# An attention and FFN kernel on one Trainium2 core: the sum of x and attention output moves from GpSimd to VectorE, a product and its row sum become one VectorE instruction, two small copies move to ScalarE

## The chip, the cores and the metric

One core of a Trainium2 chip runs the whole program. The metric is the time of one execution in device microseconds (us). Five engines work side by side and meet only through semaphores: TensorE (PE in the rows, with PEld for its weight loads), VectorE (DVE), ScalarE (ACT), GpSimd (POOL) and SyncE (SP, which here only issues DMAs). Each engine runs its instructions in the order in which they are written.

## The reference, cut to what matters

x and ctx are 16 batches of 128 x 1024 in float32. Each batch goes through an attention block and then through a feed-forward block (FFN) whose input is normalised over its 1024 features:

```python
x = x + xattn(layernorm(x), ctx, ctx)
x = x + ffn(layernorm(x))

def ffn(h):
    query = h @ Wq.T
    ... # router scores from query, top 8 of 256 slots, attention over them: aux_out
    aux_out = aux_out @ Wvd.T @ Wvu.T
    learned = (gelu(h @ Wu1.T + bu1) @ Wu2.T + bu2)[..., 0]
    u = clip(norm_var * 0.5 + sigmoid(learned) * 2.5, 0, 5)
    gate = sigmoid(gate_w1 * clip((u - 0.5) / 1.5, 0, 1) + gate_bias)
    return h + where(gate < 0.05, 0, gate) * aux_out
```

The change touches the first half of the FFN: the sum x + xattn in the layout that TensorE needs, the product with Wu1 and Wq (one matrix of 320 columns), gelu, the weighting with Wu2 and its sum over 256 units (`learned`), and `query`.

## The kernel before

The program is written by hand, engine by engine: a loop over `PERIODS` = 19 periods of four sub-steps (i = 0 to 3) pipelines the attention over the 16 batches, and ends in the FFN. In period 17 (`B + 1`) the FFN's first half begins: `hidden_step(b)` is called on TensorE, VectorE and ScalarE for b = 0 to 7 from sub-steps of periods 17 and 18 (`early_step`), for b = 8 to 16 from a loop of its own behind the periods. Step b works on batch b with the batch before and the one after it. After step 16 comes the second half (top 8, weights, output), which the change leaves as it is.

For each batch b the first half is this chain, with the engine and the line:

- SP: `load_hx` (L422) loads x transposed into one of three buffers `hx`, `load_ho` (L428) the attention output from DRAM into one of two buffers `ho`. `load_hx(n)` waits until batch n-3 has been split (`hT_lo_done`), `load_ho(n)` until batch n-2 has been added (`h_added`). They alternate in one queue.
- GpSimd: `h_add` (L1133), hx = hx + ho, 128x1024.
- ScalarE: `hT_high` (L901) rounds hx to the matmul's format (`hT_hi`); VectorE: `hT_low` (L1304) takes the rest (`hT_lo` = hx - `hT_hi`).
- TensorE: `hidden_products` (L627), 24 matmuls of 320 columns into one half of `k_slot`.
- VectorE: `unit_bias` (L1313) scales 256 of those columns and adds bu1; `query_rows` (L1318) scales the other 64 into `q_rows`.
- TensorE: `query_transpose` (L637) turns `q_rows`; VectorE: `query_copy` (L1322) moves the result to `query`.
- ScalarE: `unit_gelu` (L905); VectorE: `unit_weights` (L1326) multiplies by Wu2; ScalarE: `unit_sum` (L909) sums the product into `learned`.

VectorE's step b is, in this order, hT_low(b+1), unit_weights(b-1), unit_bias(b), query_rows(b), query_copy(b-1). ScalarE's is hT_high(b+1), unit_gelu(b-1), `hidden_sum(b)` (L895, a 128x1024 pass over x that the output needs later), unit_sum(b-1). TensorE's is hidden_products(b), query_transpose(b-1).

Other work lies in between in steps 0 to 8: on TensorE the last products of the attention (`o_pair`, L574) and the turns of its output (`o_turn`, L585); on GpSimd `norm_scale` (L1092 to L1100) and small chains for the normalisation (`rstd2_pow`, L1120 to L1127); on VectorE `residual` (L1291) and `statistics` (L1297) of the last three batches; later the split of Wvu (`WvuT_hi` on VectorE, L1503; `WvuT_lo` on GpSimd, L1205), and on ScalarE a logarithm that needs another function table (L921).

Before that, in period 16, VectorE, ScalarE, GpSimd and TensorE end the softmax of q: `q_shift` (L1258, L1264), exponent on ScalarE (L811), `q_reciprocal` (L1271, L1275), `q_scale` on GpSimd (L1081), `q_turn` on TensorE (L527).

Of the kernel before, what the change touches and what calls it, by code (L numbers as in the profile page):

```python
# [57 lines left out]
def attention_ffn_kernel(nc, x, x_cols, ctx_rows, ctx_cols, WqT_raw, WkT_raw, Wv_rows, WoT_rows, bo_row, g_row, Wuq_cols,  # L58
# [3 lines left out]
    with ctx:  # L62
# [284 lines left out]
        gelu_weighted = sem("gelu_weighted")  # L347
# [32 lines left out]
        def has(b):  # L380
            return 0 <= b < B
# [397 lines left out]
        def _(act):  # L779
# [127 lines left out]
            def unit_sum(b, k):  # L907
                act.wait_ge(gelu_weighted, b + 1)
                nc.scalar.activation(units[:, k, :], units[:, k, :], ACT.Identity,  # L909
                                     accum_out=learned[:, b, :]).then_inc(learned_done, 1)  # L910

            def hidden_step(b):
                if b + 1 < B:
                    hT_high(b + 1, (b + 1) % 2)
                if has(b - 1):
                    unit_gelu(b - 1, (b - 1) % 2)
                if has(b):
                    hidden_sum(b)
# [3 lines left out]
                if 0 < b < B:  # L922
                    unit_sum(b - 1, (b - 1) % 2)
# [110 lines left out]
            for i in range(1, B + 2):  # L1034
                if has(i - 1):
                    softmax_exp(i - 1, (i - 1) % 2)
                if i == 1:
                    unit_sum(B - 1, (B - 1) % 2)
# [16 lines left out]
        def _(pool):  # L1055
# [73 lines left out]
            def h_add(b):  # L1129

                pool.wait_ge(hx_in[b % HX], 16 * (b // HX + 1))
                pool.wait_ge(ho_in[b % 2], 16 * (b // 2 + 1))
                nc.gpsimd.tensor_tensor(hx[:, b % HX, :], hx[:, b % HX, :], ho[:, b % 2, :], ALU.add).then_inc(h_added, 1)  # L1133

# [25 lines left out]
            for b in range(PERIODS):  # L1160
                p, o, e = b - 1, b - 2, b - 3
                for i in range(4):
# [19 lines left out]
                    if b == B and i == 2:  # L1182
                        h_add(0)
                    if b == B + 1 and i == 0:
                        h_add(1)
# [3 lines left out]
                    if early_step(b, i) >= 0:  # L1189
                        h_add(early_step(b, i) + 2)  # L1190
# [9 lines left out]
            for b in range(EARLY, B):  # L1200
                if b + 2 < B:
                    h_add(b + 2)
# [16 lines left out]
        def _(dve):  # L1219
# [80 lines left out]

            def hT_low(b, k):
# [14 lines left out]
            def query_rows(b, k):  # L1316
                wait(dve, rows_T, b - 1)
                V.tensor_scalar_mul(q_rows[:, k, 0:BOT], unit_psum(b)[:, UH:UQ], rstd2[:, b, :]).then_inc(rows_copied, 1)  # L1318

            def query_copy(b, k):  # L1320
                dve.wait_ge(rows_T, b + 1)
                V.tensor_copy(query[:, b, :], query_psum(b)).then_inc(query_done, 1)  # L1322

            def unit_weights(b, k):
                dve.wait_ge(gelu_done, b + 1)
                V.tensor_tensor(units[:, k, :], units[:, k, :], Wu2[:, :], ALU.mult).then_inc(gelu_weighted, 1)  # L1326
# [267 lines left out]
```

## Time and profile before

| what | value |
|---|---|
| runs | 633.19 us median of 3 (632.27 to 635.33) |
| the profiled execution | 632.16 us |
| its span, first to last instruction | 630.3 us |
| mean granted TensorE clock | 0.984 |
| busy: TensorE, VectorE, ScalarE, GpSimd | 590.2 us (94%), 563.4 (89%), 418.3 (66%), 471.9 (75%) |
| first product of the FFN starts | at 491.87 us |
| last product of the FFN's first half starts | at 577.92 us |

The profile gives the start and length of every instruction. A length counts from the moment at which the instruction is at the head of its engine with its semaphores fulfilled, so it can hold time in which the instruction itself can't go on. Times of places are counted from the start of the span.

### The profile page before, as it was taken

Reading aid. Unit: us, or ns where it says so; the run is one execution under the profiler, and the core shown is the slowest. Engines: PE = TensorE matmul, PEld = TensorE weight load, DVE = VectorE, ACT = ScalarE, POOL = GpSimd, SP = SyncE. Lnnn points to the kernel's source line nnn. Section 1 sums busy time; section 2 is a strip of 40 time slices with the busy share of each in tenths; the row PEclk is TensorE's granted clock in tenths of the full one; section 3 lists DMA queues with packets and bytes.
Section 4 is the critical chain, followed back from the end, with each engine's and each line's share of the span. In section 5 each row is a group of like instructions: output and inputs, shape, how many; then the busy total and the mean of one; then the engine's idle time right before and its main releaser. Section 6 shows DMA issues by size and latency. Waiting matters only on the chain.

```text
span 630.3 us, 11307 instructions
## 1 busy us (share of the span) xinstructions
PE 590.2 (94%) x3606; PEld 511.0 (81%) x3606; DVE 563.4 (89%) x722; ACT 418.3 (66%) x864; POOL 471.9 (75%) x437
## 2 busy tenths in 40 slices
PE   4999999999999999999999999999897996789896
PEld 3768888888888888888888888888776986777574
DVE  5999999999999999999999999999879449987996
ACT  5556657676767676775777676767654565466783
POOL 4953569797797979797978879797848897761394
PEclk9999999999999999999999999999999899989899
DMA  7949697978889697978787886967695875550156
GB/s 299 251 128 241 187 216 218 228 205 211 226 201 234 200 241 203 239 204 214 219 224 216 208 229 184 238 226 175 183 280 196 246 258 180 187 200 1 43 226 266
DMA packets 70441, 131.33 MB, mean 208 GB/s; under 512 B 12032, under 2 KB 44448, under 8 KB 68080
## 3 DMA queue, kind: packets, MB, share of 16 engines
q1 hardware_dynamic: 57184, 101.16, 55.1%
q10 hardware_dynamic: 12304, 27.01, 16.6%
q0 software_dynamic: 896, 2.45, 1.2%
q8 instruction: 29, 0.48, 0.4%
q14 instruction: 28, 0.23, 0.1%
HBM read 63.47 MB, written 33.55 MB: 154 GB/s over the span
## 4 chain that ended last, share of the span: by engine, by line
PE 76%; DVE 7%; issue 5%; POOL 5%; ACT 3%; DMA 2%; SPq 1%; ACTq 0%; DVEq 0%; POOLq 0%
PE ob L574 16%; PE gm L543 16%; PE q_slot L501 5%; PE k_slot L501 4%; PE q_slot L503 4%; PE k_slot L503 4%; PE k_slot L502 4%; PE q_slot L502 4%; PE turn L527 4%; PE k_slot L627 2%; PE gm L552 2%; PE turn L585 2%; POOL hx L1133 2%; DVE units L1326 2%; PE turn L747 1%
## 5 line engine op out<-in xcount | busy, mean ns | idle before, releaser
L1081 POOL TENSOR_TENSOR qs_sb<-qs_sb,qrec 128x1024 f32<-128x1024 f32 x64 | 121.8, 1903 | 82.5 <-DVE qrec L1275 82.3
L574 PEld LDWEIGHTS ob<-mt_sb,q_hd 128*128 128x128 f32 x1024 | 124.5, 194 | 6.7 <-issue 2.6
L574 PE MATMUL ob<-mt_sb,q_hd 128*128 128x128 f32 x1024 | 128.1, 279 | 1.1 <-ACT q_hd L816 1.1
L543 PE MATMUL gm<-ekT,ctxT 128*128 128x256 f32 x512 | 118.2, 379 | 0.0
L543 PEld LDWEIGHTS gm<-ekT,ctxT 128*128 128x128 f32 x512 | 96.0, 190 | 13.6
L811 ACT ACTIVATE qs_sb<-qs_sb 128x1024 f32<-128x1024 f32 x64 | 68.0, 1062 | 47.6 <-DVE qs_sb L1264 46.6
L801 ACT ACTIVATE ek<-k_slot,nkm 128x1024 f32<-128x1024 f32 x62 | 69.1, 1115 | 32.2 <-DVE nkm L1239 31.8
L1239 DVE TENSOR_REDUCE nkm<-k_slot 128x1 f32<-128x1024 f32 x62 | 74.1, 1195 | 14.6 <-PE k_slot L503 14.6
L1271 DVE TENSOR_REDUCE qsum<-qs_sb 128x16 f32<-128x1024 f32 x64 | 77.2, 1206 | 3.7 <-ACT qs_sb L811 2.8
L1264 DVE TENSOR_TENSOR qs_sb<-q_slot,qm 128x1024 f32<-128x1024 f32 x64 | 78.4, 1224 | 2.2
L1246 DVE STREAM_TRANSPOSE kt<-ek 128x1024 f32<-128x1024 f32 x64 | 79.0, 1234 | 0.0
L1258 DVE TENSOR_REDUCE qm<-q_slot 128x16 f32<-128x1024 f32 x64 | 75.9, 1186 | 0.5 <-issue 0.5
L501 PE MATMUL k_slot<-ctx_hi,WkT_hi 128*128 128x512 f32 x124 | 54.7, 441 | 8.1 <-DVE ctx_lo L1439 7.3
L627 PE MATMUL k_slot<-WuqT_hi,hT_hi 128*128 128x320 f32 x128 | 43.0, 336 | 14.0 <-issue 14.0
L501 PE MATMUL q_slot<-WqT_hi,xn_hi 128*128 128x512 f32 x128 | 52.9, 413 | 1.9 <-DVE qs_sb L1264 1.8
L1133 POOL TENSOR_TENSOR hx<-hx,ho 128x1024 f32<-128x1024 f32 x16 | 42.3, 2646 | 12.5 <-DMA ho<-o_turned 12.5
L503 PE MATMUL q_slot<-WqT_lo,xn_hi 128*128 128x512 f32 x128 | 50.3, 393 | 0.0
L502 PE MATMUL q_slot<-WqT_hi,xn_lo 128*128 128x512 f32 x128 | 50.0, 391 | 0.0
L807 ACT COPY g_sb<-gm 128x512 f32<-128x512 f32 x16 | 9.4, 591 | 60.8 <-PE gm L543 60.8
L503 PE MATMUL k_slot<-ctx_lo,WkT_hi 128*128 128x512 f32 x124 | 49.2, 397 | 0.0
L502 PE MATMUL k_slot<-ctx_hi,WkT_lo 128*128 128x512 f32 x124 | 49.1, 396 | 0.0
L1304 DVE TENSOR_TENSOR hT_lo<-hx,hT_hi 128x1024 fp32r<-128x1024 f32 x16 | 28.9, 1809 | 19.6 <-ACT hT_hi L901 19.6
(192 smaller groups left out, 1385.9 us busy)
## 6 DMA issues: line engine op xcount, KB each, us to landing
ekT<-kt SPq DMA_DIRECT2D x488, 64.0 KB, 3.1
q_turned<-qt SPq DMA_DIRECT2D x16, 1024.0 KB, 4.8
q_hd<-q_turned ACTq DMA_DIRECT2D x64, 256.0 KB, 6.2
ctx_in<-ctx_rows SPq DMA_DIRECT2D x16, 512.0 KB, 6.1
x_all<-x SPq DMA_DIRECT2D x16, 512.0 KB, 4.9
ctxT<-ctx_cols SPq DMA_DIRECT2D x16, 512.0 KB, 5.7
o_turned<-o_sb ACTq DMA_DIRECT2D x16, 512.0 KB, 3.1
hx<-x_cols SPq DMA_DIRECT2D x16, 512.0 KB, 3.5
```

The source lines that it names most:

```text
L501: nc.tensor.matmul(dst, lhs[0], rhs[0], start=True, stop=False)
L502: nc.tensor.matmul(dst, lhs[1], rhs[0], start=False, stop=False)
L503: return nc.tensor.matmul(dst, lhs[0], rhs[1], start=False, stop=True)
L543: last = nc.tensor.matmul(gm[:, cols], ctxT[:, b % 2, j, :], ekT[:, 2 * half:2 * half + 2, :, j * BLK:(j + 1) * BLK], start=(j == 0), stop ...
L574: last = nc.tensor.matmul(ob[:, (j % 4) * C:(j % 4 + 1) * C], q, mt_sb[:, b % 2, t, :], start=(t == 0), stop=(t == T - 1))
L801: nc.scalar.activation(ek[:, i % 2, :], k_psum(b, i)[:, :], ACT.Exp, bias=nkm[:, i:i + 1], accum_out=ksum[:, b % 2, i:i + 1]).then_inc(k_e ...
L1081: nc.gpsimd.tensor_tensor(e, e, qrec[:, i % 2, :].unsqueeze(2).broadcast_to([P, PAIR, DH]), ALU.mult).then_inc(q_mul, 1)
L1239: V.tensor_reduce(nkm[:, i:i + 1], k_psum(b, i)[:, :], AX, ALU.max, negate=True).then_inc(k_max, 1)
L1246: V.transpose(kt[:, i, :], ek[:, i % 2, :]).then_inc(k_T, 1)
L1258: V.tensor_reduce(qm[:, :], q, AX, ALU.max).then_inc(q_max, 1)
L1264: V.tensor_tensor(qs_sb[:, i % 2, :].rearrange("p (m d) -> p m d", d=DH), q, qm[:, :].unsqueeze(2).broadcast_to([P, PAIR, DH]), ALU.subtra ...
L1271: V.tensor_reduce(qsum[:, :], qs_sb[:, i % 2, :].rearrange("p (m d) -> p m d", d=DH), AX, ALU.add).then_inc(q_sum, 1)
```

## The change

- `h_add` is issued by VectorE, in step b behind hT_low(b+1), for batch b+2; batches 0 and 1 are added in periods 16 and 17. GpSimd no longer has it.
- `unit_weights` is `tensor_tensor_reduce`: product with Wu2 and the sum over 256 columns into `learned`. It appears as two instructions, the product and a read-out of one column. `unit_sum` on ScalarE is gone, with its semaphore.
- `query_rows` and `query_copy` are issued by ScalarE, one step later than VectorE issued them: query_rows(b-1) behind hT_high(b+1), query_copy(b-2) behind unit_gelu(b-1).

The diff, without the lines that only take the old functions away:

```diff
 # ScalarE
+            def query_rows(b, k):
+                act.wait_ge(units_biased, b + 1)
+                act.wait_ge(rstd2_done, b + 1)
+                wait(act, rows_T, b - 1)
+                nc.scalar.mul(q_rows[:, k, 0:BOT], unit_psum(b)[:, UH:UQ], rstd2[:, b, :]).then_inc(rows_copied, 1)
+
+            def query_copy(b, k):
+                act.wait_ge(rows_T, b + 1)
+                nc.scalar.copy(query[:, b, :], query_psum(b)).then_inc(query_done, 1)
 
             def hidden_step(b):
                 if b + 1 < B:
                     hT_high(b + 1, (b + 1) % 2)
                 if has(b - 1):
+                    query_rows(b - 1, (b - 1) % 2)
                     unit_gelu(b - 1, (b - 1) % 2)
+                if has(b - 2):
+                    query_copy(b - 2, b % 2)
                 if has(b):
                     hidden_sum(b)
...
-                if 0 < b < B:
-                    unit_sum(b - 1, (b - 1) % 2)
...
                 if i == 1:
-                    unit_sum(B - 1, (B - 1) % 2)
+                    query_copy(B - 1, (B - 1) % 2)
                     act.wait_ge(learned_done, B)
 # GpSimd
-                    if b == B and i == 2:
-                        h_add(0)
-                    if b == B + 1 and i == 0:
-                        h_add(1)
...
-                    if early_step(b, i) >= 0:
-                        h_add(early_step(b, i) + 2)
...
-                if b + 2 < B:
-                    h_add(b + 2)
 # VectorE
+            def h_add(b):
+
+                dve.wait_ge(hx_in[b % HX], 16 * (b // HX + 1))
+                dve.wait_ge(ho_in[b % 2], 16 * (b // 2 + 1))
+                V.tensor_tensor(hx[:, b % HX, :], hx[:, b % HX, :], ho[:, b % 2, :], ALU.add).then_inc(h_added, 1)
...
             def unit_weights(b, k):
                 dve.wait_ge(gelu_done, b + 1)
-                V.tensor_tensor(units[:, k, :], units[:, k, :], Wu2[:, :], ALU.mult).then_inc(gelu_weighted, 1)
+                V.tensor_tensor_reduce(units[:, k, :], units[:, k, :], Wu2[:, :], 1.0, 0.0, ALU.mult, ALU.add,
+                                       learned[:, b, :]).then_inc(learned_done, 1)
...
                 if b + 1 < B:
                     hT_low(b + 1, (b + 1) % 2)
+                if b + 2 < B:
+                    h_add(b + 2)
...
                 if b < B:
                     unit_bias(b, b % 2)
-                    query_rows(b, b % 2)
-                if has(b - 1):
-                    query_copy(b - 1, (b - 1) % 2)
...
                     if b == B + 1 and i == 0:
                         hT_low(0, 0)
+                        h_add(1)
...
+                    if b == B and i == 2:
+                        h_add(0)
```

VectorE's order at the first addition, in period 16: `q_shift` of sub-step 2 (qm, qs_sb), then `q_reciprocal` (qsum, qrec). Before:

```order
L1258 TENSOR_REDUCE qm<-q_slot 128x16
L1264 TENSOR_TENSOR qs_sb<-q_slot,qm 128x1024
L1271 TENSOR_REDUCE qsum<-qs_sb 128x16
L1275 RECIPROCAL qrec<-qsum 128x16
L1284 STREAM_TRANSPOSE qt<-qs_sb 128x2x4x4x32
```

And with the change:

```order
L1249 TENSOR_REDUCE qm<-q_slot 128x16
L1255 TENSOR_TENSOR qs_sb<-q_slot,qm 128x1024
L1296 TENSOR_TENSOR hx<-hx,ho 128x1024
L1262 TENSOR_REDUCE qsum<-qs_sb 128x16
L1266 RECIPROCAL qrec<-qsum 128x16
L1275 STREAM_TRANSPOSE qt<-qs_sb 128x2x4x4x32
```

The addition of batch 0 (hx<-hx,ho) has come between the two, ahead of all that VectorE still does for q.

VectorE's step 10 of the FFN, one of the steps with nothing else in them. Before:

```order
L1304 TENSOR_TENSOR hT_lo<-hx,hT_hi 128x1024
L1326 TENSOR_TENSOR units<-units,Wuq_in 128x256
L1313 SCALAR_TENSOR_TENSOR units<-k_slot,rstd,Wuq_in 128x256
L1318 TENSOR_SCALAR q_rows<-k_slot,rstd 128x64
L1322 COPY query<-q_slot 128x128
```

And with the change:

```order
L1301 TENSOR_TENSOR hT_lo<-hx,hT_hi 128x1024
L1296 TENSOR_TENSOR hx<-hx,ho 128x1024
L1315 ISA units,learned<-units,Wuq_in 128x256
L1315 ISA learned 128x1
L1310 SCALAR_TENSOR_TENSOR units<-k_slot,rstd,Wuq_in 128x256
```

The addition stands behind hT_lo, the product has its read-out behind it, and the two small copies are gone from VectorE.

ScalarE at the end of the first half (steps 15 and 16 and the first exponent of the second half, L1015). Before:

```order
L905 ACTIVATE units<-units 128x256
L1015 ACT_TABLE_LOAD
L1015 ACTIVATE w_sb,wsum<-logits,nlmax 128x256
L909 ACTIVATE units,learned<-units 128x256
L1041 ACTIVATE ga<-learned,half 128x16
```

And with the change:

```order
L910 ACTIVATE q_rows<-k_slot,rstd 128x64
L904 ACTIVATE units<-units 128x256
L914 COPY query<-q_slot 128x128
L1020 ACT_TABLE_LOAD
L1020 ACTIVATE w_sb,wsum<-logits,nlmax 128x256
L914 COPY query<-q_slot 128x128
L1046 ACTIVATE ga<-learned,half 128x16
```

Two copies stand ahead of that exponent now and one behind it, where the sum stood.

## Rows read from the trace of the kernel before

**Rows 1.** The table by stretch: engines' busy time (count), granted clock, DMA share, GB/s.

```profile
526.70:578.00 51.30, 39.58 (x234) 37.02 (x234) 44.98 (x67) 30.96 (x52) 29.93 (x20) 0.93 0.44 154
...
526.68:530.40 3.72, 3.72 (x26) 3.59 (x25) 3.23 (x4) 1.24 (x3) 3.39 (x5) 1.00 0.61 170
...
534.10:539.30 5.20, 5.18 (x25) 5.14 (x25) 5.20 (x7) 2.90 (x5) 2.38 (x1) 0.67 0.54 207
...
551.00:556.20 5.20, 5.16 (x25) 5.16 (x25) 4.47 (x5) 2.70 (x5) 5.20 (x3) 0.67 0.56 202
```

**Rows 2.** Instructions grouped by line, 526.7 to 578 us: count, busy, mean ns, idle before.

```profile
L627 PE MATMUL k_slot<-WuqT_hi,hT_hi 128*128 128x320 f32 x73 | 25.0, 342 | 11.7 <-issue 11.7
...
L1304 DVE TENSOR_TENSOR hT_lo<-hx,hT_hi 128x1024 fp32r<-128x1024 f32 x9 | 17.1, 1894 | 4.2 <-ACT hT_hi L901 4.2
...
L1326 DVE TENSOR_TENSOR units<-units,Wuq_in 128x256 f32<-128x256 f32 x10 | 13.0, 1297 | 0.5 <-ACT units L905 0.5
...
L901 ACT CAST hT_hi<-hx 128x1024 fp32r<-128x1024 f32 x9 | 9.3, 1037 | 1.9 <-POOL hx L1133 1.9
L1313 DVE SCALAR_TENSOR_TENSOR units<-k_slot,rstd,Wuq_in 128x256 f32<-128x256 f32 x10 | 4.7, 475 | 0.5 <-PE k_slot L627 0.5
L909 ACT ACTIVATE units<-units 128x256 f32<-128x256 f32 x10 | 4.2, 416 | 20.4 <-DVE units L1326 20.4
...
L1322 DVE COPY query<-q_slot 128x128 f32<-128x128 f32 x10 | 2.8, 277 | 0.0
...
L909 ACT ACTIVATION_READ_ACCUMULATOR units<-units 128x1 f32 x10 | 1.9, 187 | 0.0
...
L921 ACT ACT_TABLE_LOAD x1 | 1.3, 1283 | 0.0
```

**Rows 3.** TensorE's instructions in order of time: start, length, idle before.

```profile
534.12 0.38 PE L627 MATMUL k_slot<-WuqT_hi,hT_hi 128*128 128x320 f32 x1 [3.58 <-issue]
```

**Rows 4.** The same view for VectorE, then GpSimd, at two places.

```profile
530.69 3.33 DVE L1304 TENSOR_TENSOR hT_lo<-hx,hT_hi 128x1024 fp32r<-128x1024 f32 x1 [0.77 <-ACT hT_hi L901]
...
562.00 2.63 DVE L1326 TENSOR_TENSOR units<-units,Wuq_in 128x256 f32<-128x256 f32 x1
...
530.60 2.35 POOL L1133 TENSOR_TENSOR hx<-hx,ho 128x1024 f32<-128x1024 f32 x1
...
561.49 2.86 POOL L1133 TENSOR_TENSOR hx<-hx,ho 128x1024 f32<-128x1024 f32 x1 [2.43 <-DMA ho<-o_turned]
```

**Rows 5.** The chain of waits, 574 to 590 us: start, length, engine and line.

```profile
576.20 1.72 PE turn L643 x4
577.92 3.52 PE k_slot L627 x24
...
585.05 0.42 PE turn L737 x2
```

**Rows 6.** The same timeline, other work of steps 7 to 10: VectorE, GpSimd.

```profile
535.07 1.21 DVE L1291 TENSOR_TENSOR x_all<-turn,x_all 128x1024 f32<-128x1024 f32 x1
...
540.28 1.27 DVE L1297 BATCH_NORM_STATS2 st<-x_all 128x6 f32<-128x512 f32 x2
...
543.08 1.22 DVE L1304 TENSOR_TENSOR hT_lo<-hx,hT_hi 128x1024 fp32r<-128x1024 f32 x1
...
553.14 2.57 POOL L1205 TENSOR_TENSOR WvuT_lo<-Wuq_in,WvuT_hi 128x1024 fp32r<-128x1024 f32 x1
```

**Rows 7.** The same timeline at the first addition: VectorE, GpSimd, TensorE.

```profile
480.07 1.22 DVE L1271 TENSOR_REDUCE qsum<-qs_sb 128x16 f32<-128x1024 f32 x1 [1.34 <-ACT qs_sb L811]
...
477.99 1.90 POOL L1081 TENSOR_TENSOR qs_sb<-qs_sb,qrec 128x1024 f32<-128x1024 f32 x1
...
486.24 1.09 PE L527 MATMUL turn<-ident,qs_sb 128*128 128x128 f32 x8 [2.60 <-DVE x_all L1291]
```

**Rows 8.** Lines again, 491.9 to 582 us: all products of the first half.

```profile
L627 PE MATMUL k_slot<-WuqT_hi,hT_hi 128*128 128x320 f32 x128 | 43.0, 336 | 14.0 <-issue 14.0
```

**Rows 9.** DMA issues, 526.7 to 578 us: count, KB, median us to landing.

```profile
ho<-o_turned SPq DMA_DIRECT2D x7, 512.0 KB, 4.2
```

More of the change, by code:

```diff
@@ L346, in attention_ffn_kernel @@
         gelu_done = sem("gelu_done")
-        gelu_weighted = sem("gelu_weighted")
         learned_done = sem("learned_done")
@@ L905, in unit_gelu @@
                 nc.scalar.activation(units[:, k, :], units[:, k, :], ACT.Gelu_apprx_tanh).then_inc(gelu_done, 1)
[L907 to L910, printed above, removed]
+            def query_rows(b, k):
[6 more added lines that the diff above has]
+                nc.scalar.copy(query[:, b, :], query_psum(b)).then_inc(query_done, 1)
             def hidden_step(b):
@@ L1127, in rstd2_pow @@
                 nc.gpsimd.tensor_scalar(one_rstd2[:, b, :], rstd2[:, b, :], 1.0, None, ALU.add).then_inc(one_rstd2_done, 1)
[L1129 to L1133, printed above, removed]
             nc.gpsimd.memset(half_neg[:, :], -0.5).then_inc(consts, 1)
@@ L1314, in unit_bias @@
                                        ALU.mult, ALU.add).then_inc(units_biased, 1)
[L1316 to L1322, printed above, removed]
             def unit_weights(b, k):
                 dve.wait_ge(gelu_done, b + 1)
-                V.tensor_tensor(units[:, k, :], units[:, k, :], Wu2[:, :], ALU.mult).then_inc(gelu_weighted, 1)
+                V.tensor_tensor_reduce(units[:, k, :], units[:, k, :], Wu2[:, :], 1.0, 0.0, ALU.mult, ALU.add,
+                                       learned[:, b, :]).then_inc(learned_done, 1)
             def log_mean():
```

## The prediction

> **What bounds the kernel now.** I read the table by stretch first, and in it the stretch from step 6 to the end of step 14 of the FFN's first half, where every engine has work but none is full: TensorE works 39.58 of 51.30 us, VectorE 44.98 [rows 1]. The groups by line say where TensorE stands: all its idle time, 11.7 us, lies ahead of the first matmul of a product, put down to "issue" [rows 2]. That product waits for hT_lo. The longest is the 3.58 us before 534.12 [rows 3], a tenth of a us after hT_lo's end (530.69 + 3.33 = 534.02 [rows 4]). A product with its transpose takes 3.72 us without a wait, and 5.2 us in the two stretches where the granted clock is 0.67 [rows 1]: the engine ran at its lower level (1.2 GHz) for most of those products, and at the higher (2.4 GHz) where the row says 1.00. The first of the two begins right behind the wait that ends at 534.12.
>
> So hT_lo is late, and why is the point of the case. hT_low on VectorE takes 1894 ns in the mean and the product with Wu2 1297 ns, though it has a quarter of the columns [rows 2]. The timeline shows them beside h_add on GpSimd: h_add runs from 530.60 to 532.95; hT_low, at the head from 530.69, ends at 534.02, 1.07 us after h_add. Again: h_add ends at 564.35, the product with Wu2 at 564.63, 0.28 us after it [rows 4]. VectorE's instruction with two SBUF inputs does nothing until GpSimd's is through, and then needs 1.1 us (1024 columns) or 0.3 us (256). It also holds up what follows: the sum on ScalarE waits 20.4 us in all for the product [rows 2], and behind that sum in ScalarE's order stands the next hT_high, for which the next hT_low waits. The ring hT_high, hT_low, product, sum, hT_high sets the pace, not TensorE.
>
> **The change, part by part.**
>
> h_add on VectorE. The trace has no such addition there; the nearest row is hT_low, same shape, two SBUF inputs, 1.1 us of its own [rows 4]; the far end is GpSimd's 2.35. I take 1.1. What it removes is the collision: GpSimd has no large work left in most steps.
>
> The fused product. Nothing in the trace is like it. The low end is the plain product, 0.3 us [rows 4]; the near high end adds to the 0.3 a whole pass of the length of ScalarE's sum with its read-out, 0.416 + 0.187 [rows 2], 0.9 in all. I take 0.5, the plain product with a read-out like ScalarE's, since the list of instructions has just these two. A far worse price is a rival below. ScalarE's wait for the product goes with the sum.
>
> VectorE's step is then 1.1 + 1.1 + 0.5 + 0.48 (unit_bias) = 3.2 us, ScalarE's about what it was: 30.96 / 10 = 3.1 us [rows 1, 2], less 0.6 for the sum, plus two copies at no more than VectorE's 0.28 each [rows 2]. Both are below TensorE's 3.72. The ring that is left, hT_high 1.04, hT_low 1.1, h_add 1.1, is 3.3 with its hand-overs: below it as well. I cost the two copies on ScalarE at nothing: query_rows(b-1) stands behind the hT_high that the next product needs anyway, and hT_low takes longer than the copy. That cover goes where ScalarE is late, below.
>
> So the steady step is TensorE's, 3.72. From the start of product 6 (526.68) to that of product 15 (577.92) [rows 1, 5] it was 51.24 us. Nine products are 33.5, with the 1.72 of the scores [rows 5] 35.2. The waits of 11.7, two products at the lower clock (1.5 each) and 1.3 of small gaps make up the rest. In the changed kernel TensorE will still wait where VectorE, with 0.5 us of slack a step, has other work:
> - step 8, behind residual, 1.21 [rows 6]: 0.7 us;
> - step 9, behind the statistics, whose chain runs from 540.28 to 543.08, 2.8 us [rows 6]: 2.3 us;
> - step 11, where GpSimd's WvuT_lo, 2.57 [rows 6], stops VectorE as h_add did: 2.3 us;
> - steps 13 and 14, where ScalarE loads a function table twice, 1.28 each [rows 2], and the logarithm's mean is formed: 0.7 each.
>
> That is 6.7; the stretch is 41.9 and the gain 9.3. Whether the lower clock comes back is open: one of its two came behind a wait of 3.58 [rows 3], and mine are 2.3. At worst it adds 1.5 twice, at best nothing.
>
> The entry. h_add(0) now stands ahead of q_reciprocal. VectorE was idle there for 1.34 us until 480.07, but GpSimd's q_scale runs until 479.89 [rows 7] and holds the addition off; it ends at 481.0, and q_reciprocal starts 0.9 us late. Behind it in VectorE's order stand the last q_shift and residual, for which TensorE already waits 2.60 us at 486.24 [rows 7]: TensorE is 0.9 us late into the FFN. Some comes back: of the waits for hT_lo (14.0 in the whole half, 11.7 in the stretch [rows 2, 8]) 2.3 us lie in steps 0 to 5. I expect 0.6 back, since behind them ScalarE's squares of the last batch and GpSimd's norm_scale, which o_turn awaits, are hardly earlier. Net +0.3 at product 6, between -1.4 (all back) and +0.9 (none).
>
> The exit. The second half's first transpose starts 3.6 us after the last product ends (585.05 [rows 5]). ScalarE's two copies ahead of the exponent delay it by some 0.45; the copy behind it takes the place of VectorE's. I take +0.2, between 0 and +0.8. From there on nothing is changed. GpSimd's queue loses the additions alone; its norm_scale of batch 14 comes earlier, and nobody waits for that.
>
> The queues: SP's loads wait for hT_low(n-3) and h_add(n-2), both now in VectorE's order. A load of ho lands 4.2 us after its issue [rows 9], and its buffer is free two steps less an addition before it is needed, 2 x 3.72 - 1.1 = 6.3. It fits, with 2.1 to spare; but an addition that waits for a load would now stop all of VectorE, where it stopped GpSimd alone.
>
> Sum: -9.3 + 0.3 + 0.2 = -8.8. The profiled execution took 632.16 us, 1.0 under the median of 633.19; against the median the forecast is **624.4 us**. With the bounds (0.3 to 0.9 for the fused product, clock, entry, exit) this case spans 620.5 to 629.
>
> **The rivals.**
>
> *TensorE is the bound throughout.* VectorE may catch up on the four places, since a late hT_lo costs only what exceeds the product that runs meanwhile. Then the 6.7 us of waits go too: 624.4 - 6.7 = 617.7. For it: hT_low is ready more than a us before TensorE needs it in a plain step. Against: GpSimd's WvuT_lo holds VectorE for longer than that.
>
> *VectorE is simply full.* The Trainium skill, "Perfetto Trace Analysis", section "Optimizing Scalar/DVE Operations", warns that GpSimd and VectorE share an SBUF read port, so that moving work between the two might not help. As a mechanism of this kernel, in rows: VectorE is busy 44.98 of the 51.30 us [rows 1]; nine additions at 1.22 [rows 6] add 11.0, ten pairs of copies take away 5.5, ten read-outs add 1.9 [rows 2]: 52.4, which is 1.1 more than the stretch, so 633.19 + 1.1 = 634.3, no change. Against it: the 44.98 holds the waits for GpSimd, (1.894 - 1.1) x 9 + (1.297 - 0.3) x 10 = 17 us [rows 2, 4], which end with the collision. The trace speaks against that rule here, as the shared time itself shrinks (2.4 us on GpSimd becomes 1.1 on VectorE).
>
> *Slower: the fused instruction is dear.* It stands in the middle of VectorE's step, ahead of unit_bias, which frees TensorE's target. The other three take 2.7 us, the step before was (51.24 - 1.72) / 9 = 5.5, so it decides from 2.8 us on. At 4 us, ten times the product, a step is 6.7: nine of them and the scores are 62.0, 10.8 over before, 644 us. Nothing in the trace excludes it, as no instruction of this kind runs there; against it, every VectorE pass over 256 columns that the rows show takes 0.3 to 0.5.
>
> **How the numbers follow.** A difference of 0.5%, 3.2 us here, is about what a measurement of this kernel can tell from no change. The forecast's case gets 0.64, TensorE as the bound 0.14, VectorE full 0.12 (within 0.5%), the dear instruction 0.10 (slower). Faster by over 0.5% is 0.64 + 0.14 = 0.78, within 0.12, slower 0.10. The range takes in the first two cases with their bounds and a part of the third: 617 to 631.
>
> **What would show it.** In the changed profile hT_low and h_add should each last 1.2 us where GpSimd is quiet, the fused pair under 0.7, and TensorE's products should follow every 3.7 us in steps 10, 12 and 15, with waits of some 2.3 us ahead of products 9 and 11. q_reciprocal should start 0.9 us later than 480.07, and product 15 near 569. The forecast is wrong if VectorE waits for ho inside a step, if the fused instruction takes over 1 us, or if ScalarE's hT_high is late behind its copies.

## The result, and the profile after

The changed kernel takes **623.65 us** in the median of four runs (621.67 to 626.23), the kernel before 632.73 beside it: a ratio of 0.985, 95% interval 0.981 to 0.990, so faster by 1.5%, with an interval that stays clear of 1. The forecast was 624.4. Run once more later (after_again, below), it took 622.05 where the kernel before took 632.4.

First the page of the changed kernel, its line of busy times over the whole span.

```profile
span 621.5 us, 11307 instructions
...
PE 587.3 (94%) x3606; PEld 508.6 (82%) x3606; DVE 560.0 (90%) x722; ACT 416.5 (67%) x864; POOL 435.3 (70%) x421
```

The span fell from 630.3 to 621.5 us. To see where, a few marks in TensorE's and VectorE's timelines are compared. "Product n" is the first matmul of `hidden_products(n)`, and q_reciprocal(15,1) is batch 15, sub-step 1. The last point ahead of anything that the change touches is q_reciprocal(15,1), at 473.75 before; product 15 began at 577.36 (the chain [rows 5] has 577.92 for it; what counts here is the same view for both kernels). Both from the timeline of the kernel before:

```profile
473.75 1.21 DVE L1271 TENSOR_REDUCE qsum<-qs_sb 128x16 f32<-128x1024 f32 x1
...
577.36 0.71 PE L627 MATMUL k_slot<-WuqT_hi,hT_hi 128*128 128x320 f32 x1
```

The same marks in the timeline of the changed kernel, with the start of product 6 and the products that had to wait:

```profile
476.04 1.22 DVE L1262 TENSOR_REDUCE qsum<-qs_sb 128x16 f32<-128x1024 f32 x1
...
528.44 0.39 PE L626 MATMUL k_slot<-WuqT_hi,hT_hi 128*128 128x320 f32 x1
...
541.87 0.38 PE L626 MATMUL k_slot<-WuqT_hi,hT_hi 128*128 128x320 f32 x1 [1.94 <-issue]
551.16 0.39 PE L626 MATMUL k_slot<-WuqT_hi,hT_hi 128*128 128x320 f32 x1 [0.77 <-DVE hT_lo L1301]
559.01 0.39 PE L626 MATMUL k_slot<-WuqT_hi,hT_hi 128*128 128x320 f32 x1 [0.25 <-issue]
563.18 0.38 PE L626 MATMUL k_slot<-WuqT_hi,hT_hi 128*128 128x320 f32 x1 [0.30 <-issue]
...
568.20 0.71 PE L626 MATMUL k_slot<-WuqT_hi,hT_hi 128*128 128x320 f32 x1
```

| part of the span | before, us | after, us | difference |
|---|---|---|---|
| start to q_reciprocal(15,1) | 473.75 | 476.04 | +2.29 |
| from there to product 6 (526.68, 528.44) | 52.93 | 52.40 | -0.53 |
| product 6 to product 15 | 50.68 | 39.76 | -10.92 |
| product 15 to the end | 52.94 | 53.30 | +0.36 |
| sum (span) | 630.3 | 621.5 | -8.8 |

All of the gain lies in the stretch that the prediction named. The 2.29 us ahead of it are no effect that can be pinned to the change (last section).

The table by stretch of the changed kernel, to be held against [rows 1] (columns as there):

```profile
528.44:568.20 39.76, 35.57 (x232) 33.60 (x232) 35.27 (x64) 29.25 (x52) 8.66 (x10) 1.00 0.59 196
```

And of add_alone, from product 6 to product 15 as well:

```profile
527.55:571.00 43.45, 37.62 (x232) 35.12 (x232) 38.49 (x73) 29.46 (x51) 7.75 (x10) 0.96 0.58 182
```

GpSimd's 29.93 us have become 8.66 in the changed kernel. VectorE is busy 35.27, nearly 10 us less than its 44.98, although it took on the additions. Some 5.5 of that are the copies that left (2.8 for `query_copy` [rows 2], 2.7 for `query_rows`); the rest is what waits that counted as work gave back, after the additions had been paid for. The kernel with the addition moved and nothing else (add_alone, below) shows that by itself: 38.49 us busy in the same part of the program, with the copies still on VectorE. The granted clock is 1.00 throughout, the higher level of 2.4 GHz; the two products at 0.67 are gone. The groups by line of the same stretch show it per instruction, against [rows 2]:

```profile
L626 PE MATMUL k_slot<-WuqT_hi,hT_hi 128*128 128x320 f32 x72 | 22.9, 318 | 3.4 <-issue 2.5 <-DVE hT_lo L1301 0.8
...
L1296 DVE TENSOR_TENSOR hx<-hx,ho 128x1024 f32<-128x1024 f32 x9 | 13.2, 1464 | 0.0
...
L1301 DVE TENSOR_TENSOR hT_lo<-hx,hT_hi 128x1024 fp32r<-128x1024 f32 x9 | 11.0, 1223 | 2.6 <-ACT hT_hi L900 2.6
L900 ACT CAST hT_hi<-hx 128x1024 fp32r<-128x1024 f32 x9 | 9.4, 1048 | 11.2 <-DVE hx L1296 11.2
...
L1315 DVE CUSTOM_DVE_ANT_0 units<-units,Wuq_in 128x256 f32<-128x256 f32 x10 | 4.2, 417 | 0.0
```

hT_low fell from 1894 to 1223 ns in the mean, the product from 1297 to 417 though it now forms the sum as well, and TensorE's idle time ahead of products from 11.7 to 3.4 us. The new h_add has a mean of 1464 only because one of its nine took 3.43 us. That one and a quiet step, from the timeline (VectorE, then GpSimd):

```profile
545.29 3.43 DVE L1296 TENSOR_TENSOR hx<-hx,ho 128x1024 f32<-128x1024 f32 x1
...
553.31 1.23 DVE L1301 TENSOR_TENSOR hT_lo<-hx,hT_hi 128x1024 fp32r<-128x1024 f32 x1 [0.38 <-ACT hT_hi L900]
554.45 1.22 DVE L1296 TENSOR_TENSOR hx<-hx,ho 128x1024 f32<-128x1024 f32 x1
555.59 0.42 DVE L1315 CUSTOM_DVE_ANT_0 units<-units,Wuq_in 128x256 f32<-128x256 f32 x1
555.93 0.08 DVE L1315 DVE_READ_ACCUMULATOR2_ANT learned<- 128x1 f32 x1
555.93 0.48 DVE L1310 SCALAR_TENSOR_TENSOR units<-k_slot,rstd,Wuq_in 128x256 f32<-128x256 f32 x1
...
544.33 3.31 POOL L1196 TENSOR_TENSOR WvuT_lo<-Wuq_in,WvuT_hi 128x1024 fp32r<-128x1024 f32 x1 [1.35 <-DVE WvuT_hi L1495]
```

In the quiet step four instructions follow one another at 1.14, 1.14, 0.34 and some 0.4 us: VectorE's step is 3.0. At 545.29 the addition stands behind GpSimd's WvuT_lo, which ends at 547.64; the addition ends at 548.72, 1.08 later. That is the same signature as in [rows 4], the last of its kind in this stretch.

### The profile page after: what moved, and what is told of

Same layout as the page of the kernel before. It is cut to its first block, busy times and chain, and to the rows that moved or that the text cites. A ratio compares the mean times of both kernels' runs of the same rounds, so it can differ in the third digit from the quotient of the medians.

```text
span 621.5 us, 11307 instructions
## 1 busy us (share of the span) xinstructions
PE 587.3 (94%) x3606; PEld 508.6 (82%) x3606; DVE 560.0 (90%) x722; ACT 416.5 (67%) x864; POOL 435.3 (70%) x421
## 4 chain that ended last, share of the span: by engine, by line
PE 80%; DVE 9%; issue 5%; ACT 2%; DMA 2%; POOL 2%; DVEq 0%; ACTq 0%; SPq 0%; POOLq 0%
PE ob L573 18%; PE gm L542 16%; PE k_slot L626 5%; PE q_slot L500 5%; PE turn L526 4%; PE q_slot L502 4%; PE q_slot L501 4%; PE k_slot L500 4%; PE k_slot L502 4%; PE k_slot L501 4%; PE gm L551 2%; PE turn L584 2%; DVE hx L1296 1%; PE turn L746 1%; DVE qsum L1262 1%
## 5 line engine op out<-in xcount | busy, mean ns | idle before, releaser
L626 PE MATMUL k_slot<-WuqT_hi,hT_hi 128*128 128x320 f32 x128 | 41.2, 322 | 4.0 <-issue 3.1
L856 ACT ACTIVATE junk<-o_sb 128x128 f32<-128x128 f32 x128 | 37.6, 297 | 5.5 <-issue 5.5
L526 PE MATMUL turn<-ident,qs_sb 128*128 128x128 f32 x256 | 34.4, 279 | 6.1 <-DVE x_all L1282 3.4
```

Of the source, the lines that this page charges most:

```text
L626: last = nc.tensor.matmul(dst[:, 0:UQ], hT[a][:, k, j, :], WuqT[c][:, j, :], start=(j == 0 and n == 0), stop=(j == J - 1 and n == 2))
```

## Experiments

**Two theories and what they say.** *The hold*: a VectorE instruction with two SBUF inputs does nothing while GpSimd's large addition runs; taking the addition off GpSimd is the gain. *The ring*: ScalarE's next hT_high stands behind ScalarE's sum, which waits for VectorE's product; breaking that by the fused instruction is the gain. *Unload*, a third: VectorE was full, and the copies that left it are the gain.

The three parts of the change were tried in all eight combinations. All comparisons are collected here. The last two columns come from TensorE's and VectorE's timelines of each kernel's one profiled execution; they leave out what happens ahead of the change. Two kernels have a second execution, and there the first of these columns agrees within 0.24 and 0.06 us; the kernels with the addition on GpSimd have one each. The granted clock is part of these differences and isn't taken apart from the waits: its mean from product 6 to 15 is 0.93 in the kernel before and in add_on_gpsimd, 0.96 in copies_alone, add_alone and copies_back_again, 0.97 in product_alone and 1.00 in all others.

| kernel | h_add | product and sum | copies | median, us | ratio to before, 95% interval | q_reciprocal(15,1) to product 15, us | product 6 to 15, us |
|---|---|---|---|---|---|---|---|
| before | GpSimd | apart | VectorE | 632.4 to 633.9 | 1 | 103.61 | 50.68 |
| copies_alone | GpSimd | apart | ScalarE | 632.81 | 1.000 (0.998 to 1.003) | 104.21 | 48.22 |
| product_alone | GpSimd | fused | VectorE | 629.89 | 0.995 (0.993 to 0.997) | 99.98 | 44.75 |
| add_on_gpsimd | GpSimd | fused | ScalarE | 631.87 | 0.998 (0.995 to 1.001) | 102.19 | 46.61 |
| add_alone | VectorE | apart | VectorE | 627.87 | 0.993 (0.990 to 0.995) | 95.64 | 43.45 |
| product_apart | VectorE | apart | ScalarE | 626.76 | 0.990 (0.987 to 0.993) | 95.45 | 43.04 |
| copies_back | VectorE | fused | VectorE | 621.43 | 0.981 (0.978 to 0.984) | 92.93 | 40.51 |
| copies_back_again | VectorE | fused | VectorE | 623.11 | 0.985 (0.982 to 0.989) | 92.69 | 40.55 |
| after | VectorE | fused | ScalarE | 623.65 | 0.985 (0.981 to 0.990) | 92.16 | 39.76 |
| after_again | VectorE | fused | ScalarE | 622.05 | 0.984 (0.981 to 0.986) | 92.22 | 39.79 |
| scratch_add | as after | | | 625.17 | 0.988 (0.983 to 0.992) | 95.19 | 43.07 |
| scratch_memset | as after | | | 622.42 | 0.984 (0.979 to 0.988) | 91.80 | 39.51 |
| better | as after | | | 618.99 | 0.979 (0.976 to 0.983) | 89.36 | 36.64 |
| better_copies_back | VectorE | fused | VectorE | 619.39 | 0.979 (0.977 to 0.981) | 91.05 | 37.40 |

**add_alone.** The kernel before with h_add moved to VectorE, at the places where the changed kernel has it, and nothing else.

```diff
...
-                nc.gpsimd.tensor_tensor(hx[:, b % HX, :], hx[:, b % HX, :], ho[:, b % 2, :], ALU.add).then_inc(h_added, 1)
...
+                V.tensor_tensor(hx[:, b % HX, :], hx[:, b % HX, :], ho[:, b % 2, :], ALU.add).then_inc(h_added, 1)
...
```

> Only h_add goes to VectorE; the product stays a multiply on VectorE and a sum on ScalarE, the copies of q stay on VectorE. Theory (the hold: a VectorE instruction with two SBUF inputs stands still while GpSimd's large add runs): the adds on GpSimd were the whole loss, VectorE's step is 3.0 + 0.2 + 0.2 = about 3.4 us, below TensorE's 3.72, so the time is 624 to 628 us and products 6 to 15 take 39 to 43 us. Rival 'ring' (what counts is that ScalarE's hT_high stands behind its own sum, which waits for VectorE's product): the ring stays, so 629 to 633 us. Rival 'unload' (VectorE was simply full, the two copies that leave it are the gain): VectorE carries 1.1 us more a step, so 633 us or more.

The move alone takes 8.0 us (103.61 - 95.64) off the part from q_reciprocal(15,1) to product 15, of the 11.4 to 11.5 of the whole change. The hold is the larger part, "unload" is out. But the range of the time was met only at its end, 627.87, the stretch missed its 39 to 43 us with 43.45, and the steps tell why: products 11 to 14 each follow at 4.2 to 4.4 us (10 to 12 start at 548.94, 553.14, 557.35), not at TensorE's pace. One round of it in the timeline (VectorE, then ScalarE):

```profile
551.82 1.23 DVE L1296 TENSOR_TENSOR hT_lo<-hx,hT_hi 128x1024 fp32r<-128x1024 f32 x1 [0.72 <-ACT hT_hi L901]
552.96 1.22 DVE L1291 TENSOR_TENSOR hx<-hx,ho 128x1024 f32<-128x1024 f32 x1
554.10 0.42 DVE L1318 TENSOR_TENSOR units<-units,Wuq_in 128x256 f32<-128x256 f32 x1
...
556.03 1.23 DVE L1296 TENSOR_TENSOR hT_lo<-hx,hT_hi 128x1024 fp32r<-128x1024 f32 x1 [0.73 <-ACT hT_hi L901]
...
554.55 0.42 ACT L909 ACTIVATE units<-units 128x256 f32<-128x256 f32 x1 [1.31 <-DVE units L1318]
...
554.97 1.03 ACT L901 CAST hT_hi<-hx 128x1024 fp32r<-128x1024 f32 x1
```

Each row of the ring starts within 0.1 us of the end of the one before it: hT_low 551.82, h_add 552.96, product 554.10, ScalarE's sum 554.55, hT_high 554.97, and hT_low again at 556.03. No instruction of this round is stretched, VectorE idles 0.73 us, and still a round takes 4.21 us. The ring is there, as a second limit under the hold. A third effect of the move, that the addition itself lasts 1.22 us on VectorE and 2.35 or more on GpSimd, has no run of its own; in the kernel before, ScalarE's hT_high waited 1.9 us in all for GpSimd's addition in this stretch [rows 2], so its share is probably small.

**product_alone.** The kernel before with the fused instruction in place of the multiply; ScalarE's sum goes.

```diff
...
-                V.tensor_tensor(units[:, k, :], units[:, k, :], Wu2[:, :], ALU.mult).then_inc(gelu_weighted, 1)
+                V.tensor_tensor_reduce(units[:, k, :], units[:, k, :], Wu2[:, :], 1.0, 0.0, ALU.mult, ALU.add,
+                                       learned[:, b, :]).then_inc(learned_done, 1)
```

> Only the product with Wu2 and its sum become one VectorE instruction; h_add stays on GpSimd, the copies stay on VectorE. Theory of the hold: hT_low, product or both still stand still for 2 to 2.4 us a step behind GpSimd's add, so 628 to 633 us. Rival 'ring': ScalarE no longer waits for VectorE's product before hT_high, so 624 to 627 us, and products 6 to 15 take at most 44 us though hT_lo or the product still last 2 us or more. Rival 'unload': no change, 632 to 634 us.

629.89 us: the hold's range, not the ring's. The broken ring is worth 3.6 us here (103.61 - 99.98), while the hold goes on. From product 6 on it is 5.9; ahead of that 2.3 are lost, as TensorE's `o_turn` waits 3.30 us for GpSimd's norm_scale, where it waited 0.74 in the kernel before. VectorE and GpSimd in this kernel's timeline:

```profile
557.31 2.62 DVE L1317 CUSTOM_DVE_ANT_0 units<-units,Wuq_in 128x256 f32<-128x256 f32 x1
...
556.42 3.23 POOL L1124 TENSOR_TENSOR hx<-hx,ho 128x1024 f32<-128x1024 f32 x1
```

The fused product, 0.42 elsewhere, ends at 559.93, 0.28 after GpSimd's addition (559.65): just as the plain product did in [rows 4].

**copies_alone.** The kernel before with q's rows and query copied by ScalarE.

```diff
...
-                V.tensor_copy(query[:, b, :], query_psum(b)).then_inc(query_done, 1)
+                nc.scalar.copy(query[:, b, :], query_psum(b)).then_inc(query_done, 1)
...
-                V.tensor_scalar_mul(q_rows[:, k, 0:BOT], unit_psum(b)[:, UH:UQ], rstd2[:, b, :]).then_inc(rows_copied, 1)
+                nc.scalar.mul(q_rows[:, k, 0:BOT], unit_psum(b)[:, UH:UQ], rstd2[:, b, :]).then_inc(rows_copied, 1)
```

> Only the copies of q's rows and of query go to ScalarE. Theory of the hold: they read PSUM and are short, VectorE's held instructions stay as they are, so 631 to 634 us. Rival 'ring': ScalarE's ring gets 0.5 us longer a step, so 633 to 637 us. Rival 'unload': VectorE loses 0.4 us a step over 15 steps, so 626 to 629 us.

A ratio of 1.000: the copies alone are worth nothing that the runs can tell.

**add_on_gpsimd.** The changed kernel with h_add, and only that, back on GpSimd (the diff of add_alone, reversed).

> The changed kernel with h_add back on GpSimd (fused product and ScalarE's copies stay). Theory of the hold: the loss comes back with the add, 628 to 633 us, with hT_lo or the fused product at 2 us or more in the steps from 8 on. Rival 'ring': the ring stays broken, so 622 to 626 us. Rival 'unload': VectorE is emptier than in the changed kernel, so 622 us or less.

631.87 us, a ratio of 0.998 whose interval holds 1. Without the move of h_add the other two parts give nothing that can be told from no change, and beside product_alone the copies on ScalarE even cost 2.2 us of the part looked at (102.19 against 99.98, one execution of each). The trace shows the largest wait that they bring (TensorE, then ScalarE):

```profile
509.12 0.33 PE L636 MATMUL q_slot<-ident,q_rows 128*128 128x128 f32 x1 [2.36 <-ACT q_rows L910]
...
507.81 1.04 ACT L900 CAST hT_hi<-hx 128x1024 fp32r<-128x1024 f32 x1 [3.94 <-POOL hx L1138]
508.76 0.31 ACT L910 ACTIVATE q_rows<-k_slot,rstd 128x64 f32<-128x64 f32 x1
```

query_rows now stands behind an hT_high that waits for GpSimd's addition, and TensorE's query_transpose waits for query_rows: 2.36 us, and 2.58 at the same place in copies_alone. With query_rows on VectorE that transpose doesn't wait in either of the two kernels.

**product_apart.** The changed kernel with the product taken apart again (the diff of product_alone, reversed).

> The changed kernel with the product taken apart again: a multiply on VectorE and a sum on ScalarE; h_add stays on VectorE, the copies on ScalarE. Theory of two parts (the hold was the larger part, and the ring hT_low 1.14, h_add 1.14, multiply 0.35, ScalarE's sum 0.45, hT_high 1.05 the smaller, 4.2 us a step with latencies against TensorE's 3.72): the steps from 10 on stand at 4.2 us again as with h_add alone, 626 to 629 us. Rival 'copies' (the rest of the gain comes from taking the copies off VectorE): steps of 3.5 to 3.8 us and 622 to 625 us.

626.76 us, and products 10, 11 and 12 start 4.21 us apart (549.47, 553.68, 557.89): the ring's period as add_alone had shown it, at a granted clock of 1.00. Products 13 and 14 follow at 4.77 and 4.57, in the steps with the table loads. So fusing is worth 3.2 to 3.3 us on top of the moved addition (95.45 against 92.16 and 92.22), and it is the sum's place in the ring that it pays for, not VectorE's time.

**copies_back**, and the same kernel again beside the changed one, **copies_back_again** and **after_again**. The changed kernel with the copies on VectorE (the diff of copies_alone, reversed).

> The changed kernel with q's rows and query copied by VectorE again; fused product and VectorE's h_add stay. Theory of two parts: the ring is 3.5 us and VectorE's step 3.4 us, both below TensorE's 3.72, so 622 to 625.5 us, quiet steps at 3.5 to 3.8 us. Rival 'copies': steps of 4.2 us and 626 to 629 us.

> The changed kernel once more, as the yardstick for the three that run beside it. Theory of two parts (hold and ring): the copies on ScalarE are worth nothing either way, since VectorE's step is 3.0 us with them gone and 3.4 us with them, both below TensorE's 3.72; so this kernel and the one with the copies back on VectorE come within 1 us of each other. Rival (the copies on ScalarE cost time): this one is slower by 2 us or more, as the first pair of medians, taken in different calls, had it (623.65 against 621.43).

> The kernel with the copies back on VectorE once more. Theory of two parts: within 1 us of the changed kernel that runs beside it. Rival (ScalarE's copies cost time): faster than it by 2 us or more.

Quiet steps take 3.62 us, as foretold. The first comparison (621.43, just under the expected range) looked as if ScalarE's copies cost 2 us. Side by side it is 622.05 with them on ScalarE and 623.11 on VectorE: within about 1 us, and the two intervals overlap widely. In the FFN part the changed kernel is ahead by 0.5 (92.69 - 92.22), and 1.7 in the pair of better below (91.05 - 89.36, one execution of each). That third of the change makes no difference that the times can tell.

**scratch_add.** The hold brought back by itself: the changed kernel, with one addition on GpSimd in steps 8 to 13 that nobody needs.

```diff
...
+                if b + 2 < B:
+                    pool.wait_ge(h_added, b + 3)
+                    pool.wait_ge(y_done, 1)
+                    nc.gpsimd.tensor_tensor(scratch[:, :], X[:, 0, :], X[:, 0, :], ALU.add).then_inc(scratched, 1)
+                    pool.wait_ge(scratched, b - EARLY + 1)
```

> The changed kernel with one add of 128 x 1024 on GpSimd more in each of the six steps 8 to 13, of an early row of X with itself into scratch space, started as soon as VectorE's h_add of that step is done; nobody waits for it. Theory of the hold: the fused product behind it lasts about 2.1 us instead of 0.42 in these six steps (as beside GpSimd's scaling of o once in the changed kernel), VectorE's step becomes 3.0 + 1.7 to 2.0 = about 4.9 us, and the time 627 to 631 us. Rival (GpSimd's adds and VectorE's don't disturb each other, the gain was a shorter way for h): product at 0.42 us and 622 to 625 us.

The price is there, its place was not the one expected. VectorE and GpSimd in its timeline:

```profile
550.07 0.41 DVE L1322 CUSTOM_DVE_ANT_0 units<-units,Wuq_in 128x256 f32<-128x256 f32 x1
...
551.26 2.05 DVE L1308 TENSOR_TENSOR hT_lo<-hx,hT_hi 128x1024 fp32r<-128x1024 f32 x1 [0.38 <-ACT hT_hi L902]
...
550.27 1.95 POOL L1199 TENSOR_TENSOR scratch<-x_all 128x1024 f32<-128x1024 f32 x1 [2.95 <-DVE hx L1303]
```

GpSimd starts 0.13 us after h_add's end (548.93 + 1.21 = 550.14), when the fused product is already under way and goes through in 0.41. hT_low is next: it ends at 553.31, 1.09 after the scratch addition. The stretch from product 6 to 15 grows from 39.8 to 43.07 us, and the median to 625.17 where the memset kernel beside it has 622.42. The expected 627 to 631 took 1.7 to 2.0 us for each of six additions; a held hT_low, as in four of the six steps, costs only 0.8. In the other two it is an instruction with a single input tensor in SBUF that is held: the rounding of Wvu and a scaling of 128x16, which take 0.69 and 0.23 us in the changed kernel. The first ends 0.56 us after the scratch addition beside it, the second 0.02:

```profile
545.90 1.98 DVE L1502 CAST WvuT_hi<-Wuq_in 128x1024 fp32r<-128x1024 f32 x1
...
566.30 1.08 DVE L1331 TENSOR_SCALAR varh<-logv,logrec 128x16 f32<-128x16 f32 x1
```

So the hold isn't only for VectorE's instructions with two SBUF inputs, which is all that the theory speaks of.

**scratch_memset.** The same, with GpSimd as busy but reading nothing.

```diff
...
-                    nc.gpsimd.tensor_tensor(scratch[:, :], X[:, 0, :], X[:, 0, :], ALU.add).then_inc(scratched, 1)
+                    nc.gpsimd.memset(scratch[:, :], 0.0).then_inc(scratched, 1)
...
+                    nc.gpsimd.memset(scratch[:, :], 0.0).then_inc(scratched, 1)
```

> As the kernel with the scratch add, but in each of the six steps two memsets of the same 128 x 1024 on GpSimd, which read no SBUF. Theory of the hold (it is a matter of GpSimd's reads beside VectorE's two inputs, not of GpSimd being busy): product at 0.42 us, 622 to 625 us. Rival (whatever GpSimd does slows VectorE): product and hT_low longer by as much as the memsets last, 626 us or more if they last 2 us together.

```profile
551.77 1.23 DVE L1309 TENSOR_TENSOR hT_lo<-hx,hT_hi 128x1024 fp32r<-128x1024 f32 x1 [0.38 <-ACT hT_hi L902]
...
550.77 0.95 POOL L1198 MEMSET scratch<- 128x1024 f32 x1 [1.49 <-DVE hx L1304]
551.78 0.95 POOL L1200 MEMSET scratch<- 128x1024 f32 x1
```

The second memset lies wholly within hT_low's time (timeline of VectorE, then GpSimd), and hT_low takes 1.23 us; the stretch is 39.51, as without any scratch work. For the instructions with two SBUF inputs it is not GpSimd's being busy that holds VectorE. The Trainium skill, "SBUF — State Buffer", section "SBUF: two separate sides", says that the port pair which the two engines share is locked for a whole instruction, and that a VectorE instruction with two SBUF inputs needs it only against a GpSimd instruction that reads SBUF; these two kernels agree, 2.05 us against 1.23. The scaling with one input is another case, as a memset holds it too:

```profile
564.34 1.08 DVE L1332 TENSOR_SCALAR varh<-logv,logrec 128x16 f32<-128x16 f32 x1
...
564.44 0.95 POOL L1200 MEMSET scratch<- 128x1024 f32 x1
```

It ends 0.03 us after the memset (565.39) and takes 1.08 us, as it did beside the scratch addition, in place of 0.23. That the engines meet only through semaphores, as the section on the chip has it, is therefore not true of VectorE and GpSimd.

**better**, and **better_copies_back**. Three moves at waits that the changed kernel's trace shows: WvuT_lo from GpSimd to VectorE, just ahead of unit_bias(15); the statistics of sample 15 from ahead of step 8 to behind it (their follow-up behind step 9); h_add(0) behind q_reciprocal(15,2).

```diff
...
-                if b == EARLY + 2:
-                    pool.wait_ge(wvu_hi, 1)
-                    nc.gpsimd.tensor_tensor(WvuT_lo[:, :], WvuT_in[:, :], WvuT_hi[:, :].bitcast(F32),
-                                            ALU.subtract).then_inc(wvu_lo, 1)
...
+                if b == B - 1:
+                    dve.wait_ge(wvu_hi, 1)
+                    V.tensor_tensor(WvuT_lo[:, :], WvuT_in[:, :], WvuT_hi[:, :].bitcast(F32),
+                                    ALU.subtract).then_inc(wvu_lo, 1)
...
-            statistics(B - 1)
+                if b == EARLY:
+                    statistics(B - 1)
...
-                    if b == B and i == 2:
+                    if b == B and i == 3:
                         h_add(0)
```

> The changed kernel with three moves, each at a wait that its trace shows: h_add(0) goes behind q_reciprocal(15,2); the statistics of sample 15 go behind step 8's instructions and their follow-up behind step 9's; WvuT_lo is subtracted by VectorE in step 15, where it sat idle for 1.62 us, and not by GpSimd in step 10, where it held h_add for 3.43 us. Theory of the hold and the ring: no VectorE instruction over 2 us is left between products 6 and 15, TensorE's waits ahead of products 9 and 11 go, and this stretch falls from 39.8 us (starts of products) to 36 to 37.5; the entry up to product 0 falls by 0.8 us; 618.5 to 621.5 us. Rival (VectorE's order and ScalarE set the pace there, and a wait removed is followed by the next): the stretch stays at 39 us or more, 622 to 625 us.

> The same three moves with the copies of q's rows and query on VectorE. Theory: VectorE's step is 3.4 us and in step 15 it carries 1.2 us more, so it comes within 1 us of the kernel with the three moves. Rival (ScalarE's copies cost time): faster than that by 1.5 us or more.

618.99 and 619.39 us, where the changed kernel beside them took 622.05; the ratios, 0.979 each, stand below its 0.984. The interval of better overlaps its interval a little (0.976 to 0.983 against 0.981 to 0.986), that of better_copies_back doesn't. The stretch is 36.64 and 37.40 us, where 36 to 37.5 was expected. Of better's timeline (VectorE, then TensorE):

```profile
548.98 1.22 DVE L1290 TENSOR_TENSOR hx<-hx,ho 128x1024 f32<-128x1024 f32 x1
...
572.10 1.22 DVE L1412 TENSOR_TENSOR WvuT_lo<-Wuq_in,WvuT_hi 128x1024 fp32r<-128x1024 f32 x1
573.80 0.48 DVE L1304 SCALAR_TENSOR_TENSOR units<-k_slot,rstd,Wuq_in 128x256 f32<-128x256 f32 x1 [0.48 <-PE k_slot L626]
...
549.16 0.39 PE L626 MATMUL k_slot<-WuqT_hi,hT_hi 128*128 128x320 f32 x1 [0.98 <-issue]
```

WvuT_lo takes 1.22 us at 572.10, in time that VectorE had idle (0.48 is left of it), and the addition behind hT_low(10) lasts 1.22 instead of 3.43. Product 9 no longer waits; product 10 now does, 0.98 us at 549.16, since statistics and WvuT_hi both stand behind step 8: 1.2 of the 2.2 us came back one step later. The third move failed: q_reciprocal(15,2) is on time again, but the FFN's entry isn't earlier (next section).

## Why the prediction was right

The mechanism, its place and most of its sizes were as foretold; point by point:

- **The pace without waits.** Products 7, 10 and 12 followed their predecessors at 3.62 us, where the step was put at 3.72. Eight plain steps and the one with the scores (5.02 us) are 34.0 us in place of 35.2: the floor was mis-sized by 1.2.
- **The waits left.** Starts of products minus 3.62 us: step 8 cost 0.4 (0.7 foretold), step 9 2.2 (2.3), step 11 2.05 (2.3), steps 13 and 14 0.6 each (0.7 each). In sum 5.8 against 6.7. The rival in which VectorE catches up on all of them fell here: the waits ahead of products 9 and 11 stand in the trace, 541.87 and 551.16.
- **The stretch.** 39.76 us, 41.9 foretold; against 50.68, not 51.24, as the chain's row of product 15 had been taken for its start. The gain is 10.9, 9.3 foretold.
- **The clock.** In the stretch it did not come back to its lower level behind the waits: the granted clock is 1.00. At the entry it did (below).
- **VectorE's step.** 1.14 for h_add (1.1 foretold) and 0.34 from the fused product to the next instruction (0.5, between 0.3 and 0.9). "The fused instruction is dear" needed 2.8 us there, and fell.
- **Why it works.** One mechanism was named where there are two. The ring stood in the prediction as what the held product stretches; that it would limit the step at 4.2 us by itself, once nothing is held, was not seen. Since the change fuses the product as well, the forecast didn't suffer; a forecast for the addition alone with 3.72 a step would have been too good by what the fused product adds to it, 2.7 to 3.3 us.
- **The entry.** The first half of the working held, the second didn't. The rows, VectorE, then GpSimd, then TensorE:

```profile
480.93 2.32 DVE L1296 TENSOR_TENSOR hx<-hx,ho 128x1024 f32<-128x1024 f32 x1
483.17 1.21 DVE L1262 TENSOR_REDUCE qsum<-qs_sb 128x16 f32<-128x1024 f32 x1
...
480.26 1.91 POOL L1086 TENSOR_TENSOR qs_sb<-qs_sb,qrec 128x1024 f32<-128x1024 f32 x1
...
489.33 1.97 PE L526 MATMUL turn<-ident,qs_sb 128*128 128x128 f32 x8 [3.41 <-DVE x_all L1282]
```

The first addition is held by q_scale until 482.17, as foretold, and q_reciprocal(15,2) comes 0.81 us late (0.9 foretold). So does residual behind it, and TensorE's wait for that grows from 2.60 [rows 7] to 3.41. But product 0 begins 1.7 us late, not 0.9: the other 0.88 is q_turn itself, 1.97 us for 1.09 before, as the granted clock behind the wait is 0.50 (1.2 GHz), where before it was 1.00 during q_turn and fell behind it. That isn't the move's alone: behind the same wait of 2.6 us q_turn takes 1.09, 1.36, 1.09 and 1.97 in the four kernels with the addition on GpSimd, and 1.65 to 1.97 behind the longer wait in the ten others. That h_add(1) stands ahead of q_reciprocal(15,3) was left out, and that is 1.6 us late against q_reciprocal(15,1) (15.41 us after it, before 13.78); no wait of TensorE for it shows.

By product 6 it is more than made up: -0.53, where +0.3 was foretold between -1.4 and +0.9. So 2.2 us come back where 0.6 was expected: 0.9 in the step of product 0, where the granted clock was 0.78 before and is 0.97 now, and 1.6 in TensorE's waits for hT_lo in steps 3 to 5 (2.3 before, 0.6 after); against that o_turn waits 0.5 longer. One of the prediction's signs of being wrong did show here: VectorE waits for ho inside a step, 3.15 us ahead of the addition at 499.17 and 0.40 ahead of that at 509.22. It cost nothing that shows, as TensorE has no wait in products 0 to 4.

In "better", q_reciprocal(15,2) is on time (6.32 us after (15,1), as before), and still product 0 is no earlier, since h_add(0) has only changed its place with q_reciprocal and both stand ahead of residual, for which q_turn waits:

```profile
493.94 1.97 PE L526 MATMUL turn<-ident,qs_sb 128*128 128x128 f32 x8 [3.75 <-DVE x_all L1276]
```

- **The exit.** From product 15 to the end it is 0.36 us more, foretold 0.2.
- **"VectorE is simply full"** got 0.12 and fell. The Trainium skill, "Perfetto Trace Analysis", section "Optimizing Scalar/DVE Operations", warns that moving work between GpSimd and VectorE might not help because of the port they share. Here it did, by 8 us of the part from q_reciprocal(15,1) to product 15: with the addition moved and nothing else, VectorE's busy time in the stretch fell from 44.98 [rows 1] to 38.49 us, as its waits for GpSimd had been counted in it.

That the sum came out at -8.8 in the spans, just as forecast, is luck: the stretch and the entry were 2.4 us better than foretold, and 2.3 us were lost ahead of the change in the profiled execution.

## What to carry to other kernels

An instruction that lasts longer beside another engine than alone is the thing to look for: compare each form's mean with its shortest, and see whose end it follows by its own length. Moving work onto the engine that looks fuller can then empty it. Behind such a hold look for the next ring by adding up one round of hand-overs without the stretch (here 4.2 us against TensorE's 3.6): if it is longer than the bound, the move alone gives only a part, and the edit that breaks the ring gives the rest (2.7 to 3.3 us of some 11 here).

## What the runs showed of the hardware

The hold works both ways. In the changed kernel GpSimd's one-column operation, 0.23 us long at 530.26, took 1.28 beside VectorE's hT_low, which runs from 540.55 to 541.77, and ended 0.08 after it:

```profile
540.57 1.28 POOL L1131 TENSOR_SCALAR nb<-mr 128x1 f32<-128x1 f32 x1
```

The clock can differ between executions of one and the same kernel at the same place. The granted clock from 456 to 458 us, in the tables by stretch of copies_back and then of copies_back_again:

```profile
456.00:458.00 2.00, 2.00 (x11) 1.75 (x10) 1.67 (x3) 1.16 (x2) 1.97 (x2) 1.00 0.95 394
```

```profile
456.00:458.00 2.00, 2.00 (x8) 1.57 (x8) 1.74 (x3) 0.91 (x2) 1.92 (x4) 0.72 0.96 391
```

Ahead of it TensorE has some 2 us with hardly any work in both. Where the clock falls, the way from a mark at 437 us (the subtraction in a `q_shift`, 437.26 in the changed kernel) to q_reciprocal(15,1) takes 38.6 to 38.9 us, and 36.9 to 37.3 where it does not. The changed kernel's execution is one of the former (its granted clock was 0.50 in those 2 us, the lower level of 1.2 GHz), and this part is 1.8 of its 2.29 us; the other 0.5 were there within its first 50 us. It fell in 7 of the 10 profiled kernels that have h_add on VectorE and in none of the 4 that have it on GpSimd, though nothing that differs has run by then. Whether that is chance stays open.
